# A two-layer-and-a-head network in split fp32: 8 of 20 chunk pairs of layer 1 as seven block products, 1024-column groups, weights kept split on chip

## The reference

```python
x = x.reshape(-1, 2 * F)                  # r_x is 1024 x 10240, F = 5120
x1, x2 = (x[:, :F], x[:, F:])
h1 = leaky_relu(layer_norm(x1 @ W1.T))    # W1 256 x 5120, slope 0.05
h2 = leaky_relu(layer_norm(x2 @ W1.T))
h1 = leaky_relu(layer_norm(h1 @ W2.T))    # W2 64 x 256
h2 = leaky_relu(layer_norm(h2 @ W2.T))
h = jnp.concatenate([h1, h2], axis=-1)
h = leaky_relu(layer_norm(h @ W3.T))      # W3 8 x 128
return h @ W4.T                           # W4 1 x 8
```

## Time and profile before

| | |
|---|---|
| median of 3 runs | 250.47 us (249.77 to 251.3) |
| the profiled execution: span, first to last instruction | 247.5 us |
| what the median has beside that span | 2.97 us |
| PE busy | 240.1 us, 97% |
| DVE busy | 185.4 us, 75% |
| ACT busy | 169.7 us, 69% |
| POOL busy | 8.9 us, 4% |
| DMA | 47.35 MB, 191 GB/s over the span |
| mean granted TensorE clock | 0.991 |

### The profile page before, as it was taken

The page is one execution under the profiler, slowest core; times in us unless marked ns, Lnnn a source line. Parts: engine busy times, 40 slices in busy tenths (PEclk is TensorE's granted clock), DMA queues, the critical chain, the costliest instruction groups (busy, mean ns, idle before and its releaser), DMA issues.

```text
span 247.5 us, 4093 instructions
## 1 busy us (share of the span) xinstructions
PE 240.1 (97%) x1096; PEld 196.2 (79%) x1096; DVE 185.4 (75%) x369; ACT 169.7 (69%) x320; POOL 8.9 (4%) x19
## 2 busy tenths in 40 slices
PE   7899999999999999999999999999999999999992
PEld 2588888888888888888888888888888888888882
DVE  3799999989565898777667589777756589877333
ACT  4798999876767567667568577667677756767150
POOL 2000000000000300000000110000000020000002
PEclk9999999999999999999999999999999999999996
DMA  6999899975455358666624358766625545761000
GB/s 193 394 316 319 311 301 357 347 222 169 141 171 171 125 171 252 214 187 216 188 91 155 106 170 252 246 183 216 192 91 169 169 160 167 249 197 75 0 0 1
DMA packets 15270, 47.35 MB, mean 191 GB/s; under 512 B 2080, under 2 KB 2464, under 8 KB 15264
## 3 DMA queue, kind: packets, MB, share of 16 engines
q1 hardware_dynamic: 15264, 47.28, 58.3%
HBM read 47.27 MB, written 0.00 MB: 191 GB/s over the span
## 4 chain that ended last, share of the span: by engine, by line
PE 93%; DMA 2%; DVE 1%; SPq 1%; POOL 1%; issue 1%; POOLq 0%; DVEq 0%
PE acc L492 29%; PE acc L494 29%; PE acc L487 29%; PE h_ps L521 3%; DMA w_raw<-w 2%; PE h_bank L537 1%; PE var_bank L544 1%; PE h_bank L553 1%; DVE x_lo L347 0%; POOL inv L213 0%; DVE w_lo L322 0%; POOL inv L215 0%; SPq L173 0%; SPq L171 0%; SPq L180 0%
## 5 line engine op out<-in xcount | busy, mean ns | idle before, releaser
L492 PE MATMUL acc<-x_lo,w_hi 128*128 128x512 f32 x320 | 126.1, 394 | 1.2 <-DVE x_lo L347 0.8
L494 PE MATMUL acc<-x_hi,w_lo 128*128 128x512 f32 x320 | 125.7, 393 | 0.0
L244 ACT CAST x_hi<-x_raw 128x1024 fp32r<-128x1024 f32 x76 | 79.9, 1051 | 45.1 <-PE acc L494 36.6
L347 DVE TENSOR_TENSOR x_lo<-x_raw,x_hi 128x1024 fp32r<-128x1024 f32 x79 | 96.1, 1216 | 0.0
L322 DVE SCALAR_TENSOR_TENSOR w_lo<-w_raw,w_mean,w_hi 128x256 fp32r<-128x256 f32 x160 | 70.2, 480 | 30.5 <-ACT w_hi L221 29.5
L487 PE MATMUL acc<-x_hi,w_hi 128*128 128x512 f32 x320 | 88.7, 395 | 0.1
L221 ACT ACTIVATE w_hi<-w_raw,w_mean 128x256 fp32r (+1 forms) x160 | 72.5, 501 | 3.0 <-DVE w_mean L424 1.9
L492 PEld LDWEIGHTS acc<-x_lo,w_hi 128*128 128x128 f32 x320 | 60.3, 189 | 16.1 <-DVE x_lo L347 1.2
L487 PEld LDWEIGHTS acc<-x_hi,w_hi 128*128 128x128 f32 x320 | 59.7, 189 | 13.8 <-ACT x_hi L287 0.6
L494 PEld LDWEIGHTS acc<-x_hi,w_lo 128*128 128x128 f32 x320 | 60.4, 189 | 12.8
L352 DVE SCALAR_TENSOR_TENSOR a_fm<-h_fm 128x256 f32<-128x256 f32 (+2 forms) x20 | 7.8, 421 | 11.4 <-ACT h_fm L259 11.1
(11 more groups left out here) (48 smaller groups left out, 47.9 us busy)
## 6 DMA issues: line engine op xcount, KB each, us to landing
x_raw<-x SPq DMA_DIRECT2D x79, 512.0 KB, 4.2
w_raw<-w SPq DMA_DIRECT2D x19, 256.0 KB, 3.5
x_raw<-x SPq DMA_DIRECT2D x2, 256.0 KB, 3.2
w_raw<-w SPq DMA_DIRECT2D x2, 128.0 KB, 2.4
w_raw<-w SPq DMA_DIRECT2D x1, 64.0 KB, 2.9
w_sb<-w SPq DMA_DIRECT2D x2, 8.0 KB, 3.2
out<-y SPq DMA_DIRECT2D x1, 4.0 KB, 1.4
```

The costliest lines, as they stand in the source:

```text
L244: act.copy(x_hi[:, s, :], x_raw[:, s, :])
L347: dve.tensor_tensor(x_lo[:, s, :], x_raw[:, s, :], x_hi[:, s, :].bitcast(F32), ALU.subtract).then_inc(lo_ready, 1)
L492: pe.matmul(acc[:, g % 2, m, :], wh[:, c, m, :], xl[:, c, :], start=False, stop=False, skip_group_check=True)
L494: ins = pe.matmul(acc[:, g % 2, m, :], wl[:, c, m, :], xh[:, c, :], start=False, stop=True, skip_group_check=True)
```

## The change

Layer 1's columns are now two groups of 1024, each as two halves `b` of 512. The 40 chunks are 20 pairs. A pair is a 2 x 2 block product: two blocks of W1's outputs and two chunks of features on one side, two chunks and two column halves on the other. **E units** (12 of a group's 20) do its eight block products, 8 x 3 = 24 matmuls. **S units** (8 of 20) do it with seven products of sums and differences (Winograd's form of Strassen's scheme), 7 x 3 = 21 matmuls. The order is EE, eight times SE, EE.

For an S unit four sums of x are built (`two_sums`, `third_sum`, `fourth_sum`, together 2048 columns), then three raw blocks (part R, 1536 columns) and the four sums (part T, 2048 columns) are split to hi and lo. The weights' four sums are built likewise in group 0, from weights centred to `w_mid`, then split. hi and lo of all weights are kept (`ws_*`, `we_*`), so group 1 does no work on weights. x hi and lo have one buffer for each kind of part: R, T, E0 and E1. The products of S units lie in banks P1, P5, P6, P7 (and P2, P3, P4), E units add into P2, P4, P3 and Q; all 8 banks of PSUM hold one group. After the last S unit DVE combines the S banks (`seven_into`), and after the last E unit the rest (`eight_into`), into h1. Both weight means are now ACT's (L322 of the new kernel). The epilogue runs once per 1024 columns, with leaky relu on ACT, and everything is written out without loops.

The kinds and products, ACT's and DVE's new helpers, PE's S unit and the drain (the rest of the diff is plumbing):

```diff
+SEVEN = 8
+EIGHT = PAIRS - SEVEN
...
+ORDER = "EE" + "SE" * SEVEN + "EE"
...
+P1, P2, P3, P4, P5, P6, P7, Q = range(8)
+E_BANK = ((P2, P4), (P3, Q))
+A11, A12, A22, S3, S1, S2, S4 = range(7)
+RAW_PRODUCTS = ((A11, P1), (A12, P2), (S4, P3))
+SUM_PRODUCTS = ((S1, P5), (S3, P7), (S2, P6), (A22, P4))
...
+            if kind == "S":
+                wanted = [("R", 0, (0, 1, 2)), ("T", 0, (0, 1, 2, 3))]
+            elif not units:
+                wanted = [("E0", 0, (0,)), ("E0", 0, (1,)), ("E1", 1, (0, 1))]
+            elif i + 1 == len(ORDER):
+                wanted = [("T", 0, (0, 1)), ("T", 1, (0, 1))]
+            else:
+                wanted = [("E0", 0, (0, 1)), ("E1", 1, (0, 1))]
...
+            def start_w(u):
+                s, landed = w_slot(u)
+                act.wait_ge(w_landed[s], landed)
+                for c in range(2):
+                    mean(u, c)
+                if u.kind == "S" and u.nth:
+                    act.wait_ge(w_lo_ready, w_pieces(SEVENS[u.nth - 1]))
+                for c in range(2):
+                    if u.kind == "E":
+                        centre(u, c, we_hi[:, u.nth, c * N1:(c + 1) * N1]).then_inc(w_hi_ready, 1)
                     else:
...
+                        ins = centre(u, c, w_mid[:, c * N1:(c + 1) * N1])
+                if u.kind == "S":
+                    ins.then_inc(w_mid_ready, 1)
+            def end_w(u):
+                if u.kind == "S":
+                    act.wait_ge(w_sums_ready, u.nth + 1)
+                    act.copy(ws_hi[:, u.nth, :], w_mid[:, P:]).then_inc(w_hi_ready, 1)
...
+            def layer1_end(g, b):
+                for m in range(M):
+                    act.wait_ge(drained, 5 * g + 2 + 2 * b + m)
+                    act.activation(sq1[:, b, m, :], h1[:, b, m, :], ACT.Square, scale=N1 ** -0.5)\
+                        .then_inc(sq1_ready, 1)
+                for m in range(M):
+                    act.wait_ge(sq1_ready, M * (B * g + b) + m + 1)
+                    act.activation(h1[:, b, m, :], h1[:, b, m, :], ACT.Prelu, alpha=LEAK).then_inc(a1_ready, 1)
...
+            def lo(u, part):
+                dve.wait_ge(hi_ready, part.n + 1)
+                dve.tensor_tensor(lo_of(u, part), raw_of(u, part), hi_of(u, part).bitcast(F32), ALU.subtract)\
+                    .then_inc(lo_ready, 1)
...
+            def w_two_sums(u):
+                dve.wait_ge(w_mid_ready, u.nth + 1)
+                raw = w_mid[:, 0:4 * P].rearrange("p (a b n) -> p a b n", a=2, b=2)
+                a21 = w_mid[:, 0:P].rearrange("p (o n) -> p o n", o=1).broadcast_to([P, 2, P])
+                dve.tensor_tensor(w_mid[:, 4 * P:6 * P].rearrange("p (a n) -> p a n", a=2), raw[:, :, 1, :], a21,
+                                  ALU.subtract).then_inc(w_sum_step, 1)
+            def w_third_sum(u):
+                dve.wait_ge(w_sum_step, 2 * u.nth + 1)
+                dve.scalar_tensor_tensor(out=w_block(S2), in0=w_block(S1), scalar=-1.0, in1=w_block(A11),
+                                         op0=ALU.mult, op1=ALU.subtract).then_inc(w_sum_step, 1)
+            def w_fourth_sum(u):
+                dve.wait_ge(w_sum_step, 2 * u.nth + 2)
+                dve.tensor_tensor(w_block(S4), w_block(A12), w_block(S2), ALU.add).then_inc(w_sums_ready, 1)
...
+            def two_sums(u):
+                s, landed = s_slot(u)
+                dve.wait_ge(xs_landed[s], landed)
+                if u.nth:
+                    dve.wait_ge(lo_ready, SEVENS[u.nth - 1].parts[1].n + 1)
+                raw = xs_raw[:, s, :].rearrange("p (a b n) -> p a b n", a=2, b=2)
+                b12 = x_block(u, 3).rearrange("p (o n) -> p o n", o=1).broadcast_to([P, 2, NC])
+                dve.tensor_tensor(x_sum[:, 0:2 * NC].rearrange("p (a n) -> p a n", a=2), raw[:, :, 0, :], b12,
+                                  ALU.add).then_inc(two_sums_ready, 1)
+            def third_sum(u):
+                dve.wait_ge(two_sums_ready, u.nth + 1)
+                dve.tensor_tensor(x_sum[:, 2 * NC:3 * NC], x_sum[:, 0:NC], x_block(u, 2), ALU.add)\
+                    .then_inc(third_sum_ready, 1)
+            def fourth_sum(u):
+                dve.wait_ge(third_sum_ready, u.nth + 1)
+                dve.tensor_tensor(x_sum[:, 3 * NC:4 * NC], x_sum[:, 2 * NC:3 * NC], x_block(u, 1), ALU.add)\
+                    .then_inc(sums_ready, 1)
...
+            def seven_into(g, k):
+                if k == 0:
+                    dve.wait_ge(used, SEVENS[(g + 1) * SEVEN - 1].parts[1].n + 1)
+                    dve.wait_ge(p1_copied, g + 1)
+                    dve.tensor_tensor(h1[:, 1, 1, :], h1[:, 0, 0, :], acc[:, P6, :], ALU.add).then_inc(h1_step, 1)
+                if k == 1:
+                    dve.wait_ge(h1_step, 2 * g + 1)
+                    dve.tensor_tensor(h1[:, 1, 0, :], h1[:, 1, 1, :], acc[:, P5, :], ALU.add)
+                if k == 2:
+                    dve.tensor_tensor(h1[:, 0, 1, :], h1[:, 1, 1, :], acc[:, P7, :], ALU.add).then_inc(h1_step, 1)
+                if k == 3:
+                    dve.wait_ge(h1_step, 2 * g + 2)
+                    dve.tensor_tensor(h1[:, 1, 1, :], h1[:, 0, 1, :], acc[:, P5, :], ALU.add).then_inc(drained, 1)
...
+            def eight_into(g, b, m):
+                dve.wait_ge(drained, 5 * g + 1)
+                dve.wait_ge(block_done, 4 * g + 2 * b + m + 1)
+                dve.tensor_tensor(h1[:, b, m, :], acc[:, E_BANK[b][m], :], h1[:, b, m, :],
+                                  ALU.subtract if b else ALU.add).then_inc(drained, 1)
...
+            def seven(u):
+                for part, products in zip(u.parts, (RAW_PRODUCTS, SUM_PRODUCTS)):
+                    def x_of(buffers, k):
+                        return buffers[part.buffer][:, k * NC:(k + 1) * NC]
+                    def w_of(w, n):
+                        return w[:, u.nth % SEVEN, n * P:(n + 1) * P]
+                    hi_ready_for(u, part)
+                    for k, (n, bank) in enumerate(products):
+                        free(u.g, bank)
+                        multiply(u.g, bank, w_of(ws_hi, n), x_of(x_hi, k))
+                    lo_ready_for(u, part)
+                    for k, (n, bank) in enumerate(products):
+                        multiply(u.g, bank, w_of(ws_hi, n), x_of(x_lo, k))
+                        ins = multiply(u.g, bank, w_of(ws_lo, n), x_of(x_hi, k))
+                    ins.then_inc(used, 1)
...
+            def last_eight(u):
+                for b in range(B):
+                    for m in range(M):
+                        for part in u.parts:
+                            hi_ready_for(u, part)
+                            lo_ready_for(u, part)
+                            e_hi(u, part, b, m)
+                            ins = e_lo(u, part, b, m)
+                        ins.then_inc(block_done, 1)
+                pe.wait_ge(block_done, 4 * (u.g + 1))
+                pe.sem_inc(used, 2)
```

More of the change, by code:

```diff
@@ new lines, with plan @@
+P1, P2, P3, P4, P5, P6, P7, Q = range(8)
[3 more added lines that the diff above has]
+SUM_PRODUCTS = ((S1, P5), (S3, P7), (S2, P6), (A22, P4))
+@dataclass
+class Unit:
+    n: int
+    g: int
+    kind: str
+    pair: int
+    nth: int
+    parts: list
+@dataclass
+class Part:
+    n: int
+    buffer: str
+    c: int
+    blocks: tuple
+    before: int
+def plan():
+    units, latest, count = [], {}, 0
+    for g in range(GROUPS):
+        seen = {"S": 0, "E": 0}
+        for i, kind in enumerate(ORDER):
+            pair = seen[kind] + (0 if kind == "S" else SEVEN)
+            nth = seen[kind] + g * (SEVEN if kind == "S" else EIGHT)
+            seen[kind] += 1
+            if kind == "S":
[6 more added lines that the diff above has]
+                wanted = [("E0", 0, (0, 1)), ("E1", 1, (0, 1))]
+            parts = []
+            for buffer, c, blocks in wanted:
+                parts.append(Part(count, buffer, c, blocks, latest.get(buffer, 0)))
+                count += 1
+            for part in parts:
+                latest[part.buffer] = part.n + 1
+            units.append(Unit(len(units), g, kind, pair, nth, parts))
+        assert seen == {"S": SEVEN, "E": EIGHT}
+    return units
@@ L104, in rec_kernel @@
[L104 to L108, removed]
+        half_ones = sb("half_ones", [P, H])
+        minus_half = sb("minus_half", [P, B * J])
+        zeros = sb("zeros", [P, NC], BF16)
+        small = sb("small", [P, B, 40])
+        var1_inverse = sb("var1_inverse", [P, B, J])
+        var2 = sb("var2", [P, B, J])
+        var12 = sb("var12", [P, B, J])
@@ L297, in _, with mean @@
[L297 to L305 removed]
+            def mean(u, c):
+                s, landed = w_slot(u)
+                act.activation(unused[:, c, :], w_raw[:, s, c * N1:(c + 1) * N1], ACT.Copy, scale=-1.0 / N1,
+                               accum_out=w_mean[:, u.pair, c:c + 1]).then_inc(w_mean_ready, 1)
@@ new lines, in multiply, with hi_ready_for, lo_ready_for @@
+            def multiply(g, bank, w, x):
```

(12 more changed lines are left out.)

869 lines of the change are left out of this document (436 added, 433 removed).

## The result

| | before | after |
|---|---|---|
| median | 250.88 us (249.77 to 251.39, 4 runs) | 257.27 us (255.5 to 259.41, 4 runs) |
| profiled execution: span, granted clock | 247.5 us, 0.991 | 253.7 us, 0.974 |

The changed kernel is slower: ratio 1.0262, 95% interval 1.0227 to 1.0297. The forecast was 255.2 us, range 246 to 262. The profiled execution of the changed kernel took 255.50 us, so 1.8 us lie around its span of 253.7. Some executions fall in a slower state with a lower granted clock (one of these four, 259.41 us at 0.968, and two of e2's, 248.71 and 249.11 us at 0.96), and the ratios leave them out; without it the median after is 256.32 us.

The account below looks back on a forecast made before the run. TensorE held 93% of the chain; after the change DVE was to bind group 0's SE part. Terms -11.0 + 9.4 + 1.25 + 1.6 + 1.3 - 3.6 + 5.6 = +4.6 (+4.7 by positions): 250.47 + 4.7 = 255.2 us, range 246 to 262.

Parts of the forecast that it names:

- centring of W2 and W3: Unit 8's period in group 0: centring, before hidden under PE, now adds 1.25 us.
- idle in the three E units behind: End of group 0: PE waits for E0 splits and DVE's `seven_into` passes, +1.3 us (0 to 3).
- the epilogue that remains: Between groups: layer 2, variances and layer 3 take 7.2 us (5.5 to 7.2) instead of 10.8, so -3.6.
- tail: From last product to end of span: 14.1 us against 8.5, +5.6 (3.5 to 6.5).
- The mechanism: SE part of group 0: DVE's 10.98 us plus waiting for ACT give period 11.65 against PE's 10.30, +9.4 us.
- The start: Up to the first S unit's products: loads landed at 13.8, t = 0 at 16.0, PE idle 5.4 against 3.8, +1.6 us.
- The drain: Between the groups: group 0's drain runs under the first E unit, with no wait seen.
- ACT's price: ACT's passes: 0.82 ns a column, so 896 columns 0.83 us, 1536 1.37, 2048 1.79.
- A: Rival: group 0 not bound by DVE, pair takes PE's 10.30 us; 244.5 us, faster; chance 0.15.
- C: Rival: more hand-overs and a later start, 12.3 us a pair and t = 0 at 18.5; 262 us; chance 0.10.
- B: Rival: DVE binds but ACT runs ahead enough, 10.98 us a pair; 250.5 us, no change; chance 0.15.
- D: Rival: PE's clock falls in each wait, pair grows to 14.9 us, 26 more; 281 us; chance 0.04.

Follow-up runs that it names:

- E0: Not a run: the buffer for x hi and lo of one kind of part, beside R, T and E1; no time was measured for it.
- e2: Changed kernel with sums, hi and lo of S weights made for the first S unit alone; 243.38 and 244.64 us, beside two slower executions.
- e1: Changed kernel with ACT and DVE making the next E weights behind part T in S units; 251.19 us, ratio 1.0037.
- e7: Changed kernel with e1's order, e6's start, S x and weights loaded a unit earlier, last layer 2 and variances by halves; 247.31 us, ratio 0.9879.
- e11: e3 with each unit's weights loaded one unit earlier; 250.47 us, ratio 1.0007.
- e6: Changed kernel with unit 1's second half of x loaded behind the first S unit's weights and x; 255.49 us, ratio 1.0239.
- e3: Changed kernel with no S units, all pairs as eight products (960 products); 255.6 us, ratio 1.0238.
- e9: e7 with DVE's sum of the first half's squares ahead of the last bank in the last epilogue; 247.69 us, ratio 0.9912.
- e10: e9 with the three sums of the S weights made by GpSimd instead of DVE; 258.7 us, ratio 1.0348.

## Why the prediction was right, step by step

In spans, forecast 252.2, measured 253.7 (before 247.5):

| step | forecast | measured |
|---|---|---|
| first product of PE starts | 4.7 | 5.76 |
| fourth weight sum of the first S unit (t = 0) | 16.0 | 18.0 |
| first S unit's products end | 25.9 | 28.8 |
| period of a pair | 11.65 | 11.70 (DVE idle 0.60 in it, as forecast) |
| centring of W2 and W3 | +1.25 | +1.25 (one period of 12.95) |
| eighth S unit's products end | 108.7 | 111.3 |
| idle in the three E units behind | 1.3 | 1.5 |
| drain between the groups | 0 | 0.95 |
| matmul of 512 columns | 0.2289 | 0.2271 |
| the epilogue that remains | 7.2 | 5.4 |
| last product ends | 238.1 | 240.1 |
| tail | 14.1 | 13.6 |

- **The mechanism** was right: DVE binds the SE part of group 0 through ACT's list, PE waits at xt's lo (1.12 us in the trace, 1.48 by the products; 1.35 forecast). Both causes were shown singly: e1 takes the mutual wait away (0.69 a pair), e2 takes DVE's excess away. Against 11.0 us of products the pairs lost 82.45 - 7 x 45 x 0.2271 = 10.9 us of PE's time.
- **The start was mis-sized.** "Landed at 13.8" went by the rate and the bytes (which give 13.3: 0.29 MB less than at 14 us, at 414 GB/s; the other 0.5 has no row), and left out SP's order: its second E load held the queue until 7.83, the S x was issued at 8.68 and landed at 15.76. t = 0 was 2.0 us late. PE's own lateness of 0.9 behind that (low clock, below) was made good by the next pairs, as they are DVE's.
- **The drain** was wrong: the prediction has it run under the first E unit. DVE's first pass of it (129.27) stands behind an xe lo that waited 1.84 us for ACT, and ACT for x's load. PE waited 0.96.
- **Products and epilogue** came out better. A product costs 0.2271 in the unrolled kernel, not 0.2289 (that the loop is the reason wasn't tried apart): 912 of them 1.6 us less. Layer 2's 16 records took 1.88 us: the lower bound (0.111) was nearer, and the variances 1.88 and layer 3 1.67 (145.44 to 147.12) came near the 3.7 taken for both.
- **ACT's price** was misread by a little: (1.04 - 0.632)/512 is 0.80 ns a column, not 0.82. It moves no term by more than 0.03 us, and xt's cast took 1.81 us in the chain, 1.79 by the sum.
- **Partly luck:** group 0's products end 2.65 us later than forecast and the drain adds 0.95, while group 1's products (0.8), the epilogue (1.8) and the tail (0.5) came out 3.1 us shorter. Only so is the span off by no more than 1.5. About 1.0 us is left over by this count; I put it down to the ends and new starts of PE's stretches, which isn't shown.
- **Around the span** I kept 2.97 us from the median before; the profiled execution has 1.8. The other three runs have spans of 254.5 to 257.6, so the profiled execution was the fastest of the four; this spread makes the rest up to 257.27.

Of the rivals, A (10.3 a pair) and C (12.3) are out by the period. B needs e1's order. D did happen once. PE waited 1.01 us ahead of 16.1 us and 2.06 ahead of 19.27, and the clock fell (windows of PE: busy, clock, DMA share, GB/s):

```profile
18.00:19.00 1.00, 0.00 (x0) 0.78 1.08 434
19.00:20.00 1.00, 0.73 (x2) 0.50 1.13 477
...
25.00:26.00 1.00, 1.00 (x5) 0.81 0.00 0
```
Products stood 0.43 us apart until 25.4, which cost nothing in the end. In the pairs' waits of 1.12 us it stayed at 1.00 (2.4 GHz; mean 1.00 over 28 to 110 us), so D's price of 26 us didn't come. The Trainium skill, "TensorE: Matmul & The Clock Gate", section "HAM oscillation — how this bites in real kernels", says that waits for data between bursts of matmuls can throw the array back to the low clock each time: the trace agrees for the two waits of the start, and not for those of the pairs.

What stays open: how much of e7's gain over e11 is the start (e11 lacks e6's edit) was not tried apart, nor why the clock falls among the small matmuls of the tail in e1, e3, e6, e7 and e9 and not in the changed kernel's profiled execution, where it stays at 1.00 up to 247 us.

## What to carry to other kernels

Fewer products pay only as far as the engines that prepare operands keep up: sum each engine's work for one period, then walk both in-order lists once round for waits that close a circle; here 0.69 us of each 11.70 were such a circle, and moving two calls took it out. Of 10.9 us of products saved the best version kept 3.2 beside e11, which lacks e6's start. A load's time of arrival is set by what stands ahead of it in the issuing queue, not only by bytes and rate: check that first when the order of units changes.

## What the hardware showed that I had not expected

- The granted clock fell to 0.50 (1.2 GHz) in e9 at 237.4 us, in a stretch of small plain float32 matmuls without a gap in the records. In e1 it fell at 238.9, in e7 at 237.9, also among such records; in e1 the eight pairs of records of layer 3 took 3.43 us instead of 1.80.
- A record of these costs 0.117 us with 256 moving columns (16 in 1.88), 0.117 with 1 column (the variances, 16 in 1.88) and 0.111 with 128: almost nothing for the columns.
- DVE and POOL took turns so strictly that in the 5 us of e10 shown above every stretched pass can be worked out from the rows of the other engine.
- POOL's power took 1.64 us for 8 numbers a partition, 1.01 to 1.16 for 4 and 0.70 for 2.
